# The shared expert of a mixture-of-experts decoder layer: moved behind the last chunk, its results stored in four pieces, and the last layer-norm root taken by ScalarE

## The reference

```python
x = x + attention(layernorm(x))                  # self attention, 16 heads
x = x + cross_attention(layernorm(x), ctx, mask) # 77 context rows
flat = layernorm(x)                              # 2048 rows of 256
probs = softmax(flat @ gate_W)                   # 8 experts
w, idx = top_k(probs, 2); w = w / w.sum()
out = 0.5 * gelu(flat @ shared_W + shared_b)     # the shared expert
for e in range(8):
    h = gelu(flat @ W1[e] + b1[e])               # 256 -> 1024
    out = out + combine[:, e:e+1] * (h @ W2[e] + b2[e])
x = x + layernorm(out) * gamma + beta
```

## Time and profile before

| | |
|---|---|
| median of 3 runs | 881.23 us (879.92 to 881.65) |
| profiled execution, its own time | 876.42 us |
| its span, first to last instruction | 874.6 us |
| PE busy, share of the span | 764.5 us, 87% |
| DVE, ACT, POOL busy | 378.1, 398.6, 165.0 us |

### The profile page before, as it was taken

How to read it: one execution, slowest core, us unless ns; L and a number is a source line. 1 busy time by engine, 2 the same in 40 slices (tenths; PEclk the granted TensorE clock), 3 DMA queues, 4 the chain that set the end, 5 groups by cost and what they waited for, 6 DMA issues and landing times. The chain is left out here.

```text
span 874.6 us, 17874 instructions
## 1 busy us (share of the span) xinstructions
PE 764.5 (87%) x6633; PEld 439.7 (50%) x6634; DVE 378.1 (43%) x1043; ACT 398.6 (46%) x510; POOL 165.0 (19%) x125
## 2 busy tenths in 40 slices
PE   2997999999999999989899851899999999999830
PEld 1463544557444444344544430466676667666520
DVE  5770421020524515753445543444444444444337
ACT  2656889887988988335243313111111111111113
POOL 5001131010000002002044044922212221222310
PEclk9997999999999999999899866899999999999975
DMA  9688798971560500710211293554443444454443
GB/s 213 184 235 165 225 215 193 294 116 19 59 75 15 62 2 3 259 43 0 97 49 49 84 302 100 197 135 117 121 119 100 123 120 118 100 124 120 76 118 98
DMA packets 78081, 105.97 MB, mean 121 GB/s; under 512 B 9164, under 2 KB 63142, under 8 KB 77860
## 3 DMA queue, kind: packets, MB, share of 16 engines
q1 hardware_dynamic: 70716, 93.53, 41.5%
q0 software_dynamic: 7296, 11.47, 7.0%
HBM read 66.04 MB, written 38.94 MB: 120 GB/s over the span
## 5 line engine op out<-in xcount | busy, mean ns | idle before, releaser
L723 ACT ACTIVATE arena<-ps 128x1024 f32<-128x1024 f32 x256 | 241.2, 1034 | 37.5 <-PE ps L1619 36.9
L1619 PE MATMUL ps<-arena 99*32 99x512 bf16 x2048 | 165.7, 389 | 4.9 <-issue 2.4
L1596 PE MATMUL ps<-arena 128*32 128x256 f32 x2048 | 163.0, 381 | 1.2 <-issue 1.2
L1912 PE MATMUL ps<-arena 128*128 x280 | 129.7, 607 | 0.5 <-ACT arena L815 0.5
L1929 PE MATMUL ps<-arena,xh_tag 128*128 x560 | 126.9, 380 | 1.9 <-DVE xh_tag L1344 1.4
L1929 PEld LDWEIGHTS ps<-arena,xh_tag 128*128 128x128 f32 x560 | 103.7, 190 | 15.5 <-issue 2.9
L815 ACT COPY arena<-ps 128x256 f32<-128x256 f32 x35 | 13.1, 373 | 201.4 <-PE ps L1902 195.0
L647 POOL DMA_INDIRECT sums_by_row<-arena x39 | 60.2, 1544 | 216.0 <-DVE arena L1366 214.7
L1596 PEld LDWEIGHTS ps<-arena 128*32 128x32 f32 x2048 | 68.9, 111 | 51.8 <-issue 4.4
L1339 DVE TENSOR_TENSOR xh_tag<-ps,xh_tag 128x1024 f32<-128x1024 f32 x35 | 42.9, 1225 | 89.4 <-PE ps L1912 89.3
L1912 PEld LDWEIGHTS ps<-arena 128*128 128x128 f32 x280 | 51.8, 195 | 53.6 <-issue 53.6
(11 more groups left out here) (226 smaller groups left out, 813.4 us busy)
## 6 DMA issues: line engine op xcount, KB each, us to landing
xh_tag<-in_L_ffn_b SPq DMA_DIRECT2D x35, 512.0 KB, 3.8
rows_by_expert<-arena SPq DMA_DIRECT2D x9, 1950.0 KB, 18.8
arena<-in_L_ffn_W SPq DMA_DIRECT2D x16, 1024.0 KB, 9.2
arena<-k_parts SPq DMA_DIRECT2D x48, 128.0 KB
arena<-q_parts SPq DMA_DIRECT2D x48, 128.0 KB
arena<-rows_by_expert SPq DMA_DIRECT2D x35, 130.0 KB, 2.1
arena<-in_L_ffn_b SPq DMA_DIRECT2D x35, 128.0 KB
q_parts<-arena SPq DMA_DIRECT2D x8, 384.0 KB, 2.6
```

Source lines behind the costliest of these rows:

```text
L723: nc.scalar.activation(probs_of(stage, h), ps[:, 2 * (u % 2):2 * (u % 2) + 2, :].rearrange("p a n -> p (a n)"), ACT.Exp, scale=float(D) ** ...
L1596: last = nc.tensor.matmul(ps[32 * h:32 * h + 32, 4 + half, at:at + 256], v_grp[n % 2][:, kt, h, :], probs_of(stage, h)[:, 256 * part:256 * ...
L1619: last = nc.tensor.matmul(ps[c:c + 32, 2 * (u % 2) + half, :], k_stk[buf][:, h, P * st + c:P * st + c + 32], q_stk[buf][:, h, 512 * half:5 ...
L1912: last = nc.tensor.matmul(ps[:, half, :], xs_t[:, buf, k, :], w1_sb[:, bass.ds(e, 1), k, 512 * half:512 * (half + 1)].squeeze(1), start=(k ...
```

## The change

- **Gates and shared expert are parted.** `gates(ch)` multiplies only the 8 gate columns, in the same place as before, into one PSUM bank; ACT's `gate_logits` reads all four tiles' 32 logits with one copy. `x3_t` now keeps all four chunks and lies in the 16 KB of `acc`.
- **The shared expert** is eight calls `shared(ch, p)`, each for two tiles: a matmul of the identity with `shared_b` (512 columns) starts the PSUM bank, then four matmuls of 256 columns add to it. Three calls stand on PE after `add_product(3)` and ahead of `rows3(3)`, a fourth between `gates(3)` and `ranks(3)`, and four behind the counts. ACT takes their Gelus straight from PSUM into `acc` (`shared_results`, 128 x 512 at a time), all behind `pair_weights(3)`.
- **Not halved.** POOL's multiplication by 0.5 is gone: the pair weights are doubled in `place` instead, and the final layer norm adds 4e-5 where it added 1e-5, so that all sums are twice the old ones.
- **Four stores** of 512 KB on SP (`store_base`): 0, then the weights `w2` of expert 5, then 1 and 2, all ahead of the wait for the scatters; 3 behind the first two slots' loads. POOL's first add waits for all four (`base_out`).
- **POOL** no longer adds `shared_b`; it adds `ffn_b` to `x_sb` two tiles at a time, behind each of the first eight adds of results.
- **The last chunk's root** is Sqrt on ACT and a reciprocal on DVE in place of the Newton steps.
- DVE's array `ended` moves to another place, since `sgw_sb` is still read when it is written.

```diff
@@ -236,6 +235,7 @@
         acc = Region(ACC_AT).take([P, NT, D])
+        x3_t = acc.rearrange("p t f -> p (t f)").rearrange("p (c k n) -> p c k n", c=NT // CHUNK, k=KC)
         sgw_sb = Region(SGW_AT).take([P, KC, D + EXPERTS])
...
@@ -489,9 +488,19 @@
                 load_w2(e)
-            sp.wait_ge(sg_ps, NT)
+
+            sums = sums_dram[0:NT * P, :].rearrange("(p t) f -> p t f", t=NT)
+
+            def store_base(ch):
+                sp.wait_ge(sg_act, 2 * (ch + 1))
+                rows = slice(CHUNK * ch, CHUNK * (ch + 1))
+                sp.dma_start(sums[:, rows, :], acc[:, rows, :]).then_inc(base_out, 16)
+
+            store_base(0)
             sp.wait_ge(slot_ready, NT // CHUNK)
             load_w2(5)
+            store_base(1)
+            store_base(2)
...
@@ -526,6 +535,7 @@
                 load_b2(expert(j), j)
+            store_base(3)
             sp.wait_ge(xs_ps, 1)
...
@@ -629,18 +638,9 @@
                             in_=xh_tag[:, t, :], in_offset=None).then_inc(scattered, 16)
-                pool.wait_ge(sg_read, CHUNK * (ch + 1))
-                rows = acc[:, CHUNK * ch:CHUNK * (ch + 1), :]
-                nc.gpsimd.tensor_tensor(rows, rows, shared_b_sb.unsqueeze(1).to_broadcast([P, CHUNK, D]), ALU.add)\
-                    .then_inc(sh_added, 1)
-            pool.wait_ge(sg_act, NT // 4)
-            nc.gpsimd.tensor_scalar(acc, acc, 0.5, None, ALU.mult).then_inc(halved, 1)
-            pool.wait_ge(halved, 1)
-            pool.dma_start(sums_dram[0:NT * P, :].rearrange("(p t) f -> p t f", t=NT), acc).then_inc(sums_set, 16)
             nc.gpsimd.iota(row_if_run, [[P, 2 * (PAIRS - SURE)]], base=(NT + 1) * P, channel_multiplier=1).then_inc(spare_set, 1)
-            nc.gpsimd.tensor_tensor(x_sb[:, :, :], x_sb[:, :, :], ffn_b_sb.unsqueeze(1).to_broadcast([P, NT, D]),
-                                    ALU.add).then_inc(x_shifted, 1)
             pool.wait_ge(sums_zero, 16)
+            pool.wait_ge(base_out, 16 * (NT // CHUNK))
...
@@ -649,14 +649,20 @@
             for n in range(1, 2 * SURE + 2):
-                pool.wait_ge(sums_set, 16 * n)
+                if n >= 2:
+                    pool.wait_ge(sums_set, 16 * (n - 1))
                 add_result((n - 1) % 2, n, row_at[:, (n - 1) % 2:(n - 1) % 2 + 1], sums_set)
+                if n <= NT // 2:
+                    rows = x_sb[:, 2 * n - 2:2 * n, :]
+                    last = nc.gpsimd.tensor_tensor(rows, rows, ffn_b_sb.unsqueeze(1).to_broadcast([P, 2, D]), ALU.add)
+                if n == NT // 2:
+                    last.then_inc(x_shifted, 1)
             for n in range(2 * SURE + 2, 2 * PAIRS + 2):
...
             for n in range(2):
-                pool.wait_ge(sums_set, 16 * (2 * SURE + 2 + n))
+                pool.wait_ge(sums_set, 16 * (2 * SURE + 1 + n))
                 add_result(1 - n, SLOT_TILES - 1 + n, row_at[:, 1 - n:2 - n], sums_set)
...
@@ -729,21 +735,26 @@
             def turned_rows3(ch):
+                if ch == 0:
+
+                    act.wait_ge(xs_zero, 16 * 9)
+                    act.wait_ge(sums_zero, 16)
                 for p in range(2):
                     act.wait_ge(x3_ps, 2 * ch + p + 1)
-                    nc.scalar.copy(x3_t[:, :, 256 * p:256 * (p + 1)],
+                    nc.scalar.copy(x3_t[:, ch, :, 256 * p:256 * (p + 1)],
                                    ps[:, 6 + p, :].rearrange("p (k n) -> p k n", k=KC)).then_inc(x3_ready, 1)
-            def shared_results(ch):
-                if ch == 0:
-
-                    act.wait_ge(xs_zero, 16 * 9)
+            def gate_logits(ch):
                 if ch >= 1:
                     act.wait_ge(both_ready, ch)
-                for t in range(CHUNK):
-                    act.wait_ge(sg_ps, CHUNK * ch + t + 1)
-                    nc.scalar.copy(logits[:, t, :], ps[:, 6 + t % 2, D:D + EXPERTS]).then_inc(gate_read, 1)
-                    nc.scalar.copy(acc[:, CHUNK * ch + t, :], ps[:, 6 + t % 2, 0:D]).then_inc(sg_read, 1)
+                act.wait_ge(gate_ps, ch + 1)
+                nc.scalar.copy(logits.rearrange("p t e -> p (t e)"), ps[:, 6, 0:CHUNK * EXPERTS]).then_inc(gate_read, 1)
+
+            def shared_results(ch):
+                act.wait_ge(sg_ps, 2 * ch + 2)
+                for p in range(2):
+                    nc.scalar.activation(acc[:, CHUNK * ch + 2 * p:CHUNK * ch + 2 * p + 2, :],
+                                         ps[:, 2 * (ch % 2) + p, :].rearrange("p (t f) -> p t f", t=2), ACT.Gelu).then_inc(sg_act, 1)
...
@@ -797,18 +808,18 @@
                 if ch >= 1:
-                    shared_results(ch - 1)
+                    gate_logits(ch - 1)
                 if ch == 1:
...
             pair_weights(2)
+            sqrt_of_var(NT - CHUNK, NT)
             turned_rows3(3)
-            shared_results(3)
+            gate_logits(3)
             pair_weights(3)
-            for q in range(NT // 4):
-                act.wait_ge(sh_added, q + 1)
-                nc.scalar.activation(acc[:, 4 * q:4 * q + 4, :], acc[:, 4 * q:4 * q + 4, :], ACT.Gelu).then_inc(sg_act, 1)
+            for ch in range(NT // CHUNK):
+                shared_results(ch)
...
@@ -1197,7 +1208,12 @@
                 rows = slice(CHUNK * ch, CHUNK * (ch + 1))
-                inverse_root(rstd[:, rows], mv[:, rows, 1], 1e-5, CHUNK, link)
+                if ch < NT // CHUNK - 1:
+                    inverse_root(rstd[:, rows], mv[:, rows, 1], 1e-5, CHUNK, link)
+                else:
+                    nc.vector.tensor_scalar(rstd[:, rows], mv[:, rows, 1], 1e-5, None, ALU.add).then_inc(ln_var, 1)
+                    dve.wait_ge(ln_std, B + 1)
+                    link(nc.vector.reciprocal(rstd[:, rows], rstd[:, rows]))
...
@@ -1240,7 +1256,7 @@
                 dve.wait_ge(pair_ready, ch + 1)
-                link(nc.vector.tensor_scalar(over_one, over[:, rows], 1.0, None, ALU.add))
+                link(nc.vector.tensor_scalar(over_one, over[:, rows], 0.5, 0.5, ALU.mult, ALU.add))
                 link(nc.vector.reciprocal(weight, over_one))
...
@@ -1774,25 +1790,34 @@
-            def shared_and_gate(ch, p):
-
-                if p == 0:
-                    if ch == 0:
-                        pe.wait_ge(sgw_in, 32)
-                    pe.wait_ge(x3_ready, 2 * (ch + 1))
-                for t in range(2 * p, 2 * p + 2):
-                    if p == 1:
-                        pe.wait_ge(sg_read, CHUNK * ch + t - 1)
+            def gates(ch):
+
+                if ch == 0:
+                    pe.wait_ge(sgw_in, 32)
+                pe.wait_ge(x3_ready, 2 * (ch + 1))
+                for t in range(CHUNK):
                     for k in range(KC):
-                        last = nc.tensor.matmul(ps[:, 6 + t % 2, 0:D + EXPERTS], x3_t[:, k, P * t:P * (t + 1)],
-                                                sgw_sb[:, k, :], start=(k == 0), stop=(k == KC - 1))
-                    last.then_inc(sg_ps, 1)
+                        last = nc.tensor.matmul(ps[:, 6, EXPERTS * t:EXPERTS * (t + 1)], x3_t[:, ch, k, P * t:P * (t + 1)],
+                                                sgw_sb[:, k, D:D + EXPERTS], start=(k == 0), stop=(k == KC - 1))
+                last.then_inc(gate_ps, 1)
+
+            def shared(ch, p):
+
+                if ch >= 2:
+                    pe.wait_ge(sg_act, 2 * (ch - 1))
+                bank = ps[:, 2 * (ch % 2) + p, :]
+                nc.tensor.matmul(bank, ident[:, :], shared_b_sb.unsqueeze(1).to_broadcast([P, 2, D]), start=True, stop=False)
+                for t in range(2):
+                    for k in range(KC):
+                        last = nc.tensor.matmul(bank[:, D * t:D * (t + 1)], x3_t[:, ch, k, P * (2 * p + t):P * (2 * p + t + 1)],
+                                                sgw_sb[:, k, 0:D], start=False, stop=(t == 1 and k == KC - 1))
+                last.then_inc(sg_ps, 1)
...
                 pe.wait_ge(seen_ready, ch + 1)
-                pe.wait_ge(sg_read, CHUNK * (ch + 1))
+                pe.wait_ge(gate_read, ch + 1)
                 if ch == 0:
...
@@ -1870,10 +1895,8 @@
                 if ch >= 1:
-                    shared_and_gate(ch - 1, 0)
+                    gates(ch - 1)
                 turn2(n + 2)
-                if ch >= 1:
-                    shared_and_gate(ch - 1, 1)
                 if ch == 1:
...
@@ -1883,16 +1906,21 @@
             add_product(3)
+            pe.wait_ge(s2_free, 2 * NG * (NT // CHUNK))
+            for ch, p in ((0, 0), (0, 1), (1, 0)):
+                shared(ch, p)
             rows3(3)
-            shared_and_gate(3, 0)
-            shared_and_gate(3, 1)
+            gates(3)
+            shared(1, 1)
             ranks(3)
-            pe.wait_ge(sg_read, CHUNK * (NT // CHUNK))
             nc.tensor.matmul(ps[:, 6, 0:EXPERTS], ones[:, :], seen_bf[:, :], start=True, stop=False)
...
             last.then_inc(count_ps, 1)
+            for ch in range(2, NT // CHUNK):
+                for p in range(2):
```

(1 more changed line is left out.)

29 lines of the change are left out of this document (13 added, 16 removed).

## The result

The changed kernel takes 869.37 us (median of 4 runs, 868.79 to 871.45), the kernel before 880.84 us beside it (4 runs, 879.92 to 881.65): a ratio of 0.9874, with an interval of 0.9855 to 0.9894. It is faster by 1.3%, 11.5 us, where 15.0 were forecast. The profiled execution took 868.79 us, with a span of 867.0 us.

A forecast was written before the change was run, and what follows sets the result against it. PE bounds the experts' stage, so time was sought in the gates' chains and the last chunk before it. 7.1 + 5.7 + 1.3 + 0.9 = 15.0 us, 881.2 to 866.2, stated as 866.5; range 863 to 873.5.

The forecast's parts named there:

- Gates alone, in the loop: Loop's three passes: 8 columns instead of 264, 0.107 us a matmul pass; 7.1 us gained, 1.8 at the upper bound.
- dear gates: Rival: sixteen gate passes stay near 0.22 us each; gain 7.9 us, 873.3 us; chance 0.17 including paces between.
- The forecast's split: Loop: if narrowing won nothing, the three passes would still gain 0.5, 0.5 and 0.8 us, so 1.8.
- The last chunk: From add_product(3) to the choice: earlier rows3, and rows3 and gates at 2.4 GHz; 5.7 us gained.
- the allowance for a late rise: Last chunk: PE's clock may rise later than at 508 us, each microsecond costing half; 2 us allowed.
- The Sqrt: Last chunk's root: saves 1.9 us against Newton, but worth nothing here since three shared calls on PE end later.
- POOL's lock: Last chunk: POOL's add held DVE's Newton step for 2.94 us instead of 0.16; 2.8 us goes.
- The fourth call at no cost: Between gates(3) and ranks(3): a shared call of 2.7 us lies beside 2.8 us of choice; if late, ranks are late.
- The rival of PE's own queue being late: Shared calls run slow or end after the rows land; gains of 7 to 9 us, 872 to 874; chance 0.13.
- The stores at no cost: From choice to first rows' load: stores cost 0; up to 2 us lost if DMA traffic delays the last scatters.
- The first slots: Experts' first slots: 1.3 us from a DVE stall that goes, 0.9 from the first expert matmuls' clock at even odds.
- The pieces of the add: Experts' stage: eight ffn_b pieces of 1.1 us each cost 0, as DVE is busy less than half the time.

The follow-up runs named there:

- e9: The changed kernel, unchanged, run again on another chip: 870.29 us, 0.9903 of the kernel before.
- e3: The changed kernel with gates' matmuls of 248 columns instead of 8, over two PSUM banks, only the 8 logits read: 873.11 us, 0.9944 of the kernel before.
- e1: The changed kernel with the last chunk's root by DVE's Newton steps again instead of Sqrt: 867.82 us, 0.9884 of the kernel before.
- e6: The changed kernel with two shared calls ahead of rows3(3) instead of three, gates of 128 columns and Newton's root: 868.67 us (one run).
- e8: The changed kernel with POOL's ffn_b add in one piece again, ahead of its first add of results: 869.27 us (one run).
- e4: The changed kernel with the fourth shared call moved from between gates(3) and ranks(3) to behind the counts: 871.06 us, 0.9921 of the kernel before.
- e11: The changed kernel with 128-column gates, two shared calls ahead of rows3(3), late stores, and four unused matmuls behind the last shared call: 864.98 us, 0.9839 of the kernel before.
- e10: The changed kernel with 128-column gates, two shared calls ahead of rows3(3), stores 1 to 3 behind the first loads: 869.33 us, 0.9884 of the kernel before.

## Why the prediction was right, and by how much it was not

The direction held, and so did the range; the median came 2.9 us above the forecast. On another chip (e9) the same kernel gained 8.4 us and not 11.5, so the distance from the forecast is no better known than to some 3 us. The forecast's own sum has a slip of 0.1 us: its three passes, 2.4, 2.3 and 2.5, are 7.2 and not 7.1. By its own steps:

*Gates alone, in the loop: 6.35 us gained, 7.1 forecast.* The price of a narrow pass was right (1.95 us for 16; forecast 1.7 and 0.2 of latency), and dear gates are refuted. Pass 1 gained 2.77 (forecast 2.5) and pass 3 gained 2.25 (2.4). Pass 2 gained 1.33 where 2.3 was forecast. Its missing 0.9 is the clock's fall behind the gates, by the pair of kernels with and without it (32.40 and 31.49 us); with the clock held it gained 2.24. The forecast's split was not right: it left the three passes 1.8 us if nothing were won by narrowing, and e3, with 248 columns, has 3.3.

*The last chunk: 6.19 us, 5.7 forecast.* Rows3 starts 13.31 us after add_product (forecast 13.7: 503.87 to 517.6), 1.76 us lie between it and the gates (1.8), and 2.26 to the choice (2.1). The clock rose at 503.6 us, 4.1 us behind add_product's start, as in the kernel before (508.0, 4.1 behind), and held until the gates had ended, so the allowance for a late rise was not needed. The Sqrt was worth nothing here, as forecast (e1), and 1.5 us where most of it isn't covered (e6; forecast 1.9). POOL's lock is gone with its add. Of the 6.19 us, 1.83 are the earlier start of rows3, 0.88 its turning and copy at the high clock, and 3.48 the gates; e3, whose gates of 248 columns at the high clock take 3.92 us to the choice, puts 1.8 of these 3.48 down to the clock and 1.7 to the width.

*The fourth call at no cost: a step that failed.* The prediction laid 2.7 us of PE beside 2.8 of choice, which leaves room only at full clock. The clock fell in the middle of it, and the ranks were late by 1.12 us (3.90 against 2.78). Not all of it reached the first load. The load follows the end of the last scatter's instruction by 2.75 to 3.08 us where the ranks were late and by 3.60 to 3.79 where they were on time, which fits later scatters meeting less of the stores. From choice to load the changed kernel, e1 and e8 have 19.76, 19.50 and 19.41 us, and e4 and e9, in which the clock fell only after the ranks or the call stood elsewhere, have 19.20 and 19.33. That is 0.3 us on average. The rival of PE's own queue being late was true in this one call and for a fraction of its price.

*The stores at no cost: the second step that failed.* It was bounded at 2 us and taken at 0. It costs 1.3: 19.20 to 19.37 us with the stores in place and the ranks on time (six kernels), 17.97, 18.03 and 17.89 without them (three). With the fourth call's 0.3 that makes 1.6 of the 1.87 us; the rest is this profile's distance from e1 and e8. The split goes by kernels that all have the stores; late ranks without stores were not run. Nothing else in that stretch was mis-sized: the last calls ended at 532.9 us, 13.3 us after the moment at which the ranks were due by the kernel before's 2.78 us (forecast 13.2), and the Sqrt's table load ran before its wait (499.59 us against a use at 508.30).

The prediction weighed the Trainium skill's rule (ScalarE: Activation LUTs, What ACT_TABLE_LOAD costs) that a drain about as long as the load goes with it. The trace doesn't agree for a switch to Gelu: Exp's work ends at 519.81 us, the load runs from 519.84 for 1.28 us, and the first Gelu starts at 521.13, with no gap of that length on either side.

*The first slots: 0.86 us, 2.2 forecast.* The stall of 1.3 us went as forecast. The clock of the first L1940 was put at even odds of 1.9 us, a mean of 0.9, and the result was on the other side of them: 5.92 us against 5.54. PE stood idle for 5.95 us before the first rows, and the clock fell at 537.7. e11 shows that it was the idle time: with PE fed, 3.0 us from the first turning to that of the hidden rows. The pieces of the add were right at 0, but for another reason than was given. They took 1.83 to 1.87 us each, not 1.1, and none of the eight lay beside L1367 (the first ran from 559.32 to 561.19 us, and L1367 followed at 562.80); e8 shows that they were not needed for the gain either.

The Trainium skill (SBUF — State Buffer, Who interferes with whom) says that a VectorE instruction with two SBUF inputs contends with a GpSimd instruction that reads SBUF, and that one with at most one SBUF input, outside the two-port modes, does not. The kernel before agrees for the whole-array add: beside it L1339, with one input from PSUM, took its usual 1.23 us (at 561.19), and L1351, with both from SBUF, 4.57. It doesn't agree for POOL's halving, which reads SBUF too and beside which L1351 took its usual 0.21 us; the measurement decides:

```profile
546.44 10.56 POOL L637 TENSOR_SCALAR arena<-arena 128x4096 f32<-128x4096 f32 x1 [1.18 <-ACT arena L811]
...
555.41 0.21 DVE L1351 SCALAR_TENSOR_TENSOR arena<-arena 128x1 f32<-128x1 f32 x1
```

In e8 DVE had no instruction at all beside the add, so that run says nothing on the rule.

The four misses, 0.75, -0.49, 1.87 and 1.34, add up to the 3.5 us between 15.0 and 11.53. The first rows' load, named for about 532.5 us, came at 536.61: 2.0 us of that are the later start of this profile's first gates, the rest is in the misses.

## What to carry to other kernels

When work is laid beside a chain with next to nothing to spare, its price at both clock levels belongs in the sum: here a call of 2.7 us stood beside 2.8 us and took 4.5 (516.40 to 520.92 us). Stores that nothing waits for are not free while a scatter's landing is on the path (1.3 us here); put them behind the loads that wait for it. Where PE starts from idle, its first passes may run at the low clock: eight took 6.47 us behind a pause (e10) and 3.69 with PE kept at work until the rows landed (e11). And below some width fewer columns bring no more: 128 cost 0.1 us over 8 for sixteen float32 passes.
